# Gated delta-rule attention with a routed FFN: 64 weight columns in the last level's products and in the inverse's last product

## The reference, cut to what matters

```python
def step(S, inputs):
    q_t, k_t, v_t, g_t, b_t = inputs
    S = S * jnp.exp(g_t)[..., None]
    kv = jnp.einsum('bhd,bhdv->bhv', k_t, S)
    delta = b_t[..., None] * (v_t - kv)
    S = S + k_t[..., None] * delta[:, :, None, :]
    o = jnp.einsum('bhd,bhdv->bhv', q_t, S)
    return (S, o)
```

## Time and profile before

| | |
|---|---|
| median of 3 runs | 5362.73 us (5358.38 to 5371.95) |
| the profiled execution | 5360.98 us, span 5359.2 us |
| TensorE (PE) busy | 4957.4 us, 93% of the span |
| weight loads (PEld) busy | 3937.7 us, 73% |
| VectorE (DVE) busy | 3775.5 us, 70% |
| ScalarE (ACT) busy | 3289.2 us, 61% |
| GpSimd (POOL) busy | 2882.2 us, 54% |

### The profile page before, as it was taken

How to read it: one execution, slowest core, us unless ns; L and a number is a source line. 1 busy time by engine, 2 the same in 40 slices (tenths; PEclk the granted TensorE clock), 3 DMA queues, 4 the chain that set the end, 5 groups by cost and what they waited for, 6 DMA issues and landing times.

```text
span 5359.2 us, 114813 instructions
## 1 busy us (share of the span) xinstructions
PE 4957.4 (93%) x30720; PEld 3937.7 (73%) x30720; DVE 3775.5 (70%) x8897; ACT 3289.2 (61%) x7088; POOL 2882.2 (54%) x6210
## 2 busy tenths in 40 slices
PE   3999999999999999999999999999999997999999
PEld 2778787877787878787878777777777786555555
DVE  2777777777777878686877777786777784555555
ACT  2767676767676767676777767676777673111111
POOL 1766666666575757666666656666666673000000
PEclk9999999999999999999999999999999997999999
DMA  2111111111111111111111111111111111000000
GB/s 89 35 31 40 29 38 31 38 33 36 35 35 31 39 29 37 31 37 33 35 36 35 36 31 36 33 36 33 36 35 36 33 37 38 8 12 8 12 12 12
DMA packets 214188, 173.47 MB, mean 32 GB/s; under 512 B 146432, under 2 KB 164096, under 8 KB 213376
## 3 DMA queue, kind: packets, MB, share of 16 engines
q1 hardware_dynamic: 213504, 165.49, 10.9%
HBM read 119.03 MB, written 46.40 MB: 31 GB/s over the span
## 4 chain that ended last, share of the span: by engine, by line
PE 72%; issue 10%; POOL 7%; ACT 4%; DVE 3%; DMA 3%; POOLq 1%; SPq 0%; DVEq 0%; ACTq 0%
PE bank L1346 12%; PE bank L1559 9%; PE bank L1257 9%; PE bank L1368 6%; PE bank L1312 5%; PE bank L1569 4%; PE bank L1327 4%; PE bank L1394 3%; POOL rm L399 2%; POOL mul L395 2%; PE bank L1271 2%; PE bank L1409 2%; PE bank L1265 2%; DMA lx<-blocks_in 2%; PE bank L1381 2%
## 5 line engine op out<-in xcount | busy, mean ns | idle before, releaser
L376 POOL TENSOR_TENSOR kl<-kl,tot 128x256 f32<-128x256 f32 x768 | 502.1, 654 | 820.0 <-PE bank L1346 634.7
L1346 PE MATMUL bank<-kq,kl 128*128 128x128 f32 x6144 | 858.4, 282 | 71.1 <-DVE kq L854 45.0
L1346 PEld LDWEIGHTS bank<-kq,kl 128*128 128x128 f32 x6144 | 750.6, 192 | 122.5 <-issue 86.9
L1257 PE MATMUL bank<-xT,par 128*128 128x512 f32 x1536 | 771.7, 599 | 6.2 <-DVE xall L981 5.8
L399 POOL TENSOR_TENSOR rm<-rm,mul 32x14 f32<-32x14 f32 (+6 forms) x1792 | 579.1, 323 | 140.3
L395 POOL TENSOR_TENSOR mul<-pm,rm 32x14 f32<-32x14 f32 (+6 forms) x1792 | 516.4, 288 | 136.3 <-issue 36.4
L854 DVE TENSOR_TENSOR kq<-kq,tot 128x512 f32<-128x512 f32 x768 | 533.2, 694 | 0.0
L981 DVE TENSOR_TENSOR xall<-xall,bank 128x512 f32 (+1 forms) x256 | 175.7, 687 | 413.5 <-PE bank L1327 411.9
L864 DVE COPY_PREDICATED AT<-mask,bank 128x256 f32<-128x256 uint32 x896 | 466.4, 521 | 0.0
L838 DVE COPY_PREDICATED lx<-mask,bank 128x256 f32<-128x256 uint32 x512 | 296.4, 579 | 213.7 <-PE bank L1346 213.6
L356 POOL TENSOR_TENSOR rstd<-rstd,minus_half 128x4 f32<-128x4 f32 x32 | 32.3, 1008 | 739.1 <-DVE rstd L801 739.1
(11 more groups left out here) (173 smaller groups left out, 12854.0 us busy)
## 6 DMA issues: line engine op xcount, KB each, us to landing
par<-params_dram SPq DMA_DIRECT2D x128, 519.0 KB, 3.5
blocks_out<-lx SPq DMA_DIRECT2D x128, 256.0 KB, 2.0
lx<-blocks_in SPq DMA_DIRECT2D x128, 256.0 KB, 2.8
xall<-x_dram SPq DMA_DIRECT2D x16, 512.0 KB, 3.8
pm<-blocks_out SPq DMA_DIRECT2D x512, 8.0 KB
blocks_in<-rm SPq DMA_DIRECT2D x512, 8.0 KB
out_dram<-xall SPq DMA_DIRECT2D x16, 512.0 KB, 2.9
lx<-ffn_dram SPq DMA_DIRECT2D x1, 3456.0 KB, 11.0
```

The source lines that it names most:

```text
L376: pool.tensor_tensor(halves(kl[:, :], w)[:, :, 0, :], src, totr.broadcast_to([P, SEQ // (2 * w), w]), ALU.mult).then_inc(s["kl_ready"], 1)
L1257: ins = pe.matmul(bank[t][:, :], par[p][:, at:at + P], chunk(xT, kt, SEQ), start=kt == 0, stop=kt == KT - 1)
L1346: ins = pe.matmul(dst[:, :, n], chunk(left, n), right[:, :, n, :, 1, :], start=True, stop=True)
```

## The change

In `level(6)` the weights are columns 0 to 63 of each chunk of `kl` in place of all 128, and the products are written to partitions 0 to 63 of `b_lvl`. `l_evict(6)` and `qk_evict(6)` become plain copies of these 64 partitions, without mask. In `t_products(6)` the weights are columns 0 to 63 of each chunk of `XW` (its filled half), the products go to partitions 0 to 63 of `b_y`, and `t_update(6)` subtracts on 64 partitions. The numbers of instructions, the moving columns (128 in `level(6)`, 64 in `t_products(6)`) and the order stay. TensorE gets a `sem_inc` ahead of each of the two groups, VectorE loses the one ahead of `qk_evict(6)`. The array shape is not given in the code; it follows from the number of weight columns.

```diff
@@ l_evict
                     after(dve, s["x_mm"], HIGH * (iB - 2) + l - LOW + 1)
+                    if l == LEVELS - 1:
+                        dve.tensor_copy(right_halves(LT[l - LOW][pB], w)[0:HALF], right[0:HALF]
+                                        ).then_inc(s["lt_done"], 1)
+                        return
                     dve.tensor_tensor(right_halves(LT[l - LOW][pB], w), right, each_chunk(mask[l][:, :], w), ALU.mult
                                       ).then_inc(s["lt_done"], 1)
@@ qk_evict
+                    if l == LEVELS - 1:
+                        dve.tensor_copy(right_halves(AT[mB][:, :], w)[0:HALF], packed(b_lvl[:, 256:512], w)[0:HALF]
+                                        ).then_inc(s["qk_ev"], 1)
+                        return
                     dve.sem_inc(s["dve_go"], 1)
                     dve.copy_predicated(right_halves(AT[mB][:, :], w), each_chunk(mask[l][:, :].bitcast(U32), w),
@@ t_update
-                    dve.tensor_tensor(tr, tr, b_y[:, 0:256].rearrange("p (m h) -> p m h", h=w),
+                    dve.tensor_tensor(tr[0:HALF], tr[0:HALF], b_y[0:HALF, 0:256].rearrange("p (m h) -> p m h", h=w),
                                       ALU.subtract).then_inc(s["tt_upd"], 1)
@@ level
-                    dst = b_lvl[:, :].rearrange("p (q n m h) -> p q n m h", q=2, n=NCH, h=w)
+                    rows = HALF if l == LEVELS - 1 else P
+                    dst = b_lvl[0:rows, :].rearrange("p (q n m h) -> p q n m h", q=2, n=NCH, h=w)
+                    if rows < P:
+                        pe.sem_inc(s["pe_go"], 1)
                     for n in range(NCH):
-                        ins = pe.matmul(dst[:, :, n], chunk(left, n), right[:, :, n, :, 1, :], start=True, stop=True)
+                        ins = pe.matmul(dst[:, :, n], left[:, n * P:n * P + rows], right[:, :, n, :, 1, :],
+                                        start=True, stop=True)
                     ins.then_inc(s["lvl_mm"], 1)
@@ t_products, level 6
+                    pe.sem_inc(s["pe_go"], 1)
                     for n in range(NCH):
-                        ins = pe.matmul(b_y[:, n * HALF:(n + 1) * HALF].rearrange("p (m h) -> p m h", h=w),
-                                        chunk(XW, n), halves(chunk(TT[p], n), w)[:, :, 1, :], start=True, stop=True)
+                        ins = pe.matmul(b_y[0:HALF, n * HALF:(n + 1) * HALF], XW[:, n * P:n * P + HALF],
+                                        TT[p][:, n * P + HALF:(n + 1) * P], start=True, stop=True)
                     ins.then_inc(s["yw_mm"], 1)
```

More of the change, by code:

```diff
@@ L179, in delta_moe @@
         fabs e_done f_read w_done nr_done ln_done t1_done t2_done decay_done sg_done
-        sums_mm tk_done raw_done rec_done sc_done rinv_done tot_step tot_done
+        sums_mm pe_go tk_done raw_done rec_done sc_done rinv_done tot_step tot_done
         kq_ready kl_ready kcopy lvl_mm lt_done low_done qk_ev at_init t_upd tt_upd
```

## The result

The changed kernel takes 5436.5 us (median of 4 runs, 5432.5 to 5441.3) where the kernel before takes 5361.3 beside it (5358.4 to 5372.0): a ratio of 1.0137 [1.0119, 1.0155], 75 us slower. The profiled execution took 5436.2 us, with a span of 5434.5. The sign and the range of the prediction hold and the size is near (+58 forecast).

The account below looks back on a forecast made before the run. TensorE was taken to bound the end of each step. Shape changes (792 ns per step) less shorter loads (337) made 455 ns, 58 us: 5361 + 58 = 5419 us, 5421 against the median; range 5317 to 5445.

Parts of the forecast that it names:

- TensorE bounds the end of the step: End of each step: a change in a TensorE group's length moves the program one for one, until another engine is late.
- Shorter loads, `t_products(6)`: In `t_products(6)`, 64-column loads cut the pitch from 111 to 56 ns: 337 ns saved per step, 43.1 us.
- Shorter loads, `level(6)`: 0: In `level(6)`, 128 moving columns still take 106 ns a pair: at most 0.1 us saved, taken as 0.
- The changed shape of the array: Four shape changes per step around the two groups: 173 ns going in, 223 coming out, 792 ns per step, 101.4 us.
- The two `sem_inc`: 0: TensorE's `sem_inc` ahead of both groups: taken as 0; without cover up to 0.3 us per step, 38 us.
- Who is late next: the gate on ACT, at most 6 us: `project_out(1)` waits for ACT's gate: 0.31 us of room for 0.337, at most 0.05 us lost, 6 us in all.
- room enough: GpSimd's product for `sums(2)` ends at 2025.82, its group starts at 2026.58, so no loss was expected.
- VectorE: "I take 0 for all three": VectorE's L842, L864 and L879: copies worth -0.04 to +0.04 us each, 64 partitions up to a halving; taken as 0.
- Sum: Whole kernel: 792 - 337 = 455 ns slower per step, 58 us, giving 5419 us, 5421 against the median.
- Rival A: Shape changes are free and only the shorter load at `t_products(6)` counts: 5318 us, 5320 against the median; chance 0.33.
- Rival B: About a draw: shape changes cost near 84 ns, or neither effect happens; 5350 to 5377 us; chance 0.15.
- D: Shape stays 128*128 with 64 columns used, so no shape change arises; time and chance counted in Rival A.

Follow-up runs that it names:

- e8: e4 with every second chunk of `level(6)` using all 128 weight columns, six changes of shape per step instead of four; 5422.0 us, 1.0125 of the kernel before.
- e9: Kernel before with only the change's two `sem_inc` on TensorE, ahead of `level(6)` and `t_products(6)`; 5341.7 us, ratio 0.9983.
- e3: Kernel before with only VectorE's two evictions of level 6 made plain copies of 64 partitions, TensorE's instructions unchanged; 5439.0 us, ratio 1.0163.
- e1: Kernel before with only `t_products(6)` and `t_update(6)` as in the change, level 6 as before; 5335.2 us, ratio 0.9971.
- e12: Changed kernel with VectorE's `kq_update(6)` moved ahead of `l_evict(6)`; 5430.7 us, 1.0153 of the kernel before.
- e13: e3 with VectorE's `kq_update(6)` moved ahead of `l_evict(6)`; 5427.0 us, 1.0148 of the kernel before.
- e2: Kernel before with only `level(6)` on 64 weight columns and the two plain copies, `t_products(6)` as before; 5451.7 us, ratio 1.0197.
- e4: Changed kernel with the masks back in both evictions of level 6, still on 64 partitions; 5438.3 us, 1.0154 of the kernel before.
- e14: Kernel before with `lt_times_t(6)` and `t_products(6)` on 64 weight columns, and VectorE's `kq_update(6)` ahead of `l_evict(6)`; 5341.1 us, ratio 0.9993.
- e11: e3 with VectorE's `qk_evict(6)` moved between `kq_update(6)` and the next two large operations; 5488.2 us, 1.0244 of the kernel before.

## Why the prediction was right, and for which part by the wrong reason

*TensorE bounds the end of the step.* Right, with its condition "until another engine is late"; what followed was the other engine, GpSimd.

*Shorter loads, `t_products(6)`.* Right. The eight pairs after, in TensorE's lines (duration ns min/median/max):

```profile
L1412 PEld LDWEIGHTS bank<-TT,lx x1024: 132/138/231, 169.8 to 4582.2; 128*64 128x64 f32 x171
```

The median load is 54 ns shorter than the 192 of the earlier trace rows, and the eight loads (0.54 us in all) give a pitch of (0.54 - 0.138) / 7 = 0.057 us; 0.056 was forecast. The Trainium skill's rule, columns divided by 1.2 GHz, gives 53 ns for 64 columns (TensorE: Matmul & The Clock Gate, LDWEIGHTS); the traces agree in size. Less the exit border, the group is 0.23 us shorter, which fits the 337 ns.

*Shorter loads, `level(6)`: 0.* Right; nothing came back there.

*The changed shape of the array.* The mechanism is there, the size was too large. The forecast was 173 ns going in and 223 coming out, 792 ns per step. Measured: `level(6)`'s two borders cost 0.21 us together, `t_products(6)`'s 0.337 - 0.08 = 0.26 if the loads gave back their 0.337, together 0.47 us, 60 us in place of 101. The load at a border does start late as forecast: the loads of `sums(0)` start at 2089.18 and come every 0.111 us, so the last matmul ahead starts near 2090.07, and L1412's first load at 2090.27, 0.2 us behind. Against the pitch of 0.111 that is 0.09 lost. What I had added, a load that nothing hides, is paid in part: the first pitch in L1412's group is 0.33 - 0.222 = 0.107 us by its first two matmuls where the others are 0.058, 0.05 more going in, and L1305's first pitch behind it is 0.165 where it was 0.115 before, 0.05 coming out in place of the 0.10 forecast. The wait itself was put too high coming out: there the load starts 0.15 us after the last matmul of L1412 (2090.88 - 2090.73). e8 gives 0.20 us for a border between single chunks, so the price isn't one number. The Trainium skill says that changing the tiling mode drains TensorE (TensorEngine Tiling (Array Packing), Key Properties); that agrees in kind with all of these borders.

*The two `sem_inc`: 0.* Right (e9).

*Who is late next: the gate on ACT, at most 6 us.* Right, ACT isn't in the new waits. (0.337 - 0.31 is 0.03 us and not 0.05, 4 us in all.) GpSimd "room enough" was the wrong look: it was asked of one product's end with its own durations as before, and not of what sets them.

*VectorE: "I take 0 for all three".* This is the step that failed. The durations were right (0.41 us in both kernels), and as work they cost nothing. But with the new evictions GpSimd is held 1.8 us longer beside the three operations that follow. Nothing in the prediction asked who runs beside these operations. In e3, where only the evictions differ, the cost is 1.63% (87 us); in the change it is what is left beside TensorE's own +16, some 58 us.

*Sum.* 58 forecast = 101 - 43. Measured 75 = 60 - 43 + 58. The two misses, 41 too much for the shape and 58 too little for GpSimd, nearly cancel, and that is why the total looks right: the nearness is luck. The 58 is what is left of 75, and it holds the 8 us or so that the lower clock may be worth.

*The clock.* The prediction read "at the higher level" from the slices of the earlier trace rows. A mean of 0.976 says that some 5% of the span (2 x 0.024) were at the lower one already, and the forecast had no term for a change of that share.

*Rival A* (shapes free) is wrong as a mechanism, but e1 shows its direction at `t_products(6)`, where two borders cost less than the loads give back. *Rival B*, a border near 84 ns, is the closest to TensorE's part: four borders at 0.12 us leave +16 us, a ratio of 1.003. *D* is excluded by the shape 128*64.

What stays open: why GpSimd, once caught, loses every turn until VectorE's row ends, where it gets one turn after each operation in the kernel before; whether the 64 partitions, the plain form or the instant sets the long hold off; why e12 and e13, with a shorter hold, cost as much (the estimate for the clock covers a part); how the about 11 us of the change spread that stand in no single group (the clock's 8 may be most of them); and e2's 105 us.

## What to carry to other kernels

Where VectorE and GpSimd both read SBUF, the length of an edited VectorE operation says little: put the two engines' timelines of the stretch side by side, and ask for each GpSimd operation what VectorE does at its start. An edit of an eviction (a copy of 64 partitions for a masked product of 128) can cost more than the matmul work it goes with, so each part of a change is timed alone, and two properties that an edit changes together get a run each. Halving weight columns pays only where loads set the pitch and the group is long enough: here 8 pairs save 0.34 us and two borders take 0.26.

## What the runs showed of the hardware that was not expected

A GpSimd operation of 0.22 us that starts 69 ns ahead of a row of three VectorE operations with two SBUF operands, behind an eviction of 64 partitions, is held over all three (2.03 us in the changed kernel and e4). At about 100 and 140 ns it is free behind a masked eviction of 128 partitions (0.23 in e14, 0.22 before), and held behind a plain copy of 64 from PSUM (1.47 in e13 over the two operations left, 2.11 in e3). Which property of the eviction counts is not shown. A copy inside the row doesn't end it (2.43 in e11). An operation that starts inside the first of the row waits only for that one (0.67 in e8).

The Trainium skill says of the port pair that VectorE and GpSimd share that whoever starts first gets it for the whole instruction and the other is fully blocked (SBUF — State Buffer, SBUF: two separate sides). The blocking agrees with the rows above. "Starts first" doesn't by the trace's start times: the GpSimd operations held longest are those that started ahead of VectorE's. But the trace shows when an operation is recorded to start and not when it takes the ports, and recorded spans on GpSimd are rough, so the rule isn't refuted. It speaks of one instruction, and the hold lasts over three (2.03 us) or four (2.43).

A `sem_inc` on TensorE between groups costs nothing that can be measured (e9, 0.9983). A change of the array's shape between 128*128 and 128*64 costs 0.10 to 0.13 us at the border of a group (half of 0.21 and of 0.26), and 0.20 between single chunks (e8).
